# Merging TensorE runs in a fused attention and gated linear attention kernel, with every engine's order written anew

## The reference, cut to what matters

```python
x = x + xattn(layernorm(x), ctx, indices)      # x: 4 x 1024 x 256
x = x + ffn(layernorm(x))

# xattn: 16 heads of 16, 154 keys, 64 picks of keys per query (with repetition)
kv = (c_sel @ W_kv_up.T)                       # c_sel: picked rows of x_kv @ W_kv_down.T
attn = softmax(q k / 4 over the 64 picks);  out = (attn v) @ W_out.T

# ffn: 8 heads of 64, chunked gated linear attention
q1, k1, v = x @ Wq, x @ Wk, x @ Wv
q2 = x @ Wqa @ Wqb;  k2 = softmax(x @ Wka @ Wkb over 64)       # "second" keys
gk1, gk2 = log_sigmoid(x @ Wg1a @ Wg1b + b), log_sigmoid(x @ Wg2a @ Wg2b + b)
o = gla(q1, k1, v, gk1) + sum over 4 experts of gla(q2*f, k2*f, v, gk2*m)   # top-1 router
g = x @ Wga @ Wgb
o = o * rsqrt(mean(o*o) + eps) * norm_w * (g * sigmoid(g));  out = o @ Wo
```

## Time and profile before

| | |
|---|---|
| median of 3 runs | 1136.37 us (1136.36 to 1137.0) |
| profiled execution: its own time, its span | 1137.37 us, 1135.8 us |
| granted TensorE clock, mean | 0.988 |
| PE busy (matmul records) | 1077.7 us, 95% of the span, 11840 records |
| PE weight loads | 872.7 us, 77% |
| DVE busy | 978.7 us, 86% |
| ACT busy | 933.8 us, 82% |
| POOL busy | 686.0 us, 60% |

### The profile page before, as it was taken

How to read it: one execution, slowest core, us unless ns; L and a number is a source line. 1 busy time by engine, 2 the same in 40 slices (tenths; PEclk the granted TensorE clock), 3 DMA queues, 4 the chain that set the end, 5 groups by cost and what they waited for, 6 DMA issues and landing times.

```text
span 1135.8 us, 30935 instructions
## 1 busy us (share of the span) xinstructions
PE 1077.7 (95%) x11840; PEld 872.7 (77%) x11840; DVE 978.7 (86%) x2793; ACT 933.8 (82%) x2322; POOL 686.0 (60%) x707
## 2 busy tenths in 40 slices
PE   2879999999999999999999999999999999999986
PEld 1557888887888788778888887888787788888764
DVE  5679999998899999999999998999899999998652
ACT  2578888888888888888888898888889888888761
POOL 4266555577655556766655677565557666555553
PEclk9889999999999999999999999999999999999998
DMA  5432222223222222223212222222222222121111
GB/s 155 141 124 58 72 52 57 54 70 76 67 68 52 50 57 73 62 70 86 67 43 50 57 67 71 73 71 48 63 57 61 63 68 68 44 52 48 31 32 24
DMA packets 86857, 73.83 MB, mean 65 GB/s; under 512 B 34553, under 2 KB 71743, under 8 KB 86710
## 3 DMA queue, kind: packets, MB, share of 16 engines
q1 hardware_dynamic: 86278, 70.98, 24.4%
q10 hardware_dynamic: 432, 0.89, 0.2%
HBM read 37.43 MB, written 13.94 MB: 45 GB/s over the span
## 4 chain that ended last, share of the span: by engine, by line
PE 79%; DVE 8%; DMA 3%; POOL 3%; ACT 3%; SPq 2%; issue 1%; DVEq 0%; ACTq 0%
PE F L407 8%; PE F L862 5%; PE F L810 5%; PE TM L732 5%; PE F L401 5%; PE F L873 4%; PE F L782 4%; PE F L837 4%; PE TM L739 3%; PE F L797 3%; PE F L867 3%; PE SA L720 3%; PE F L821 3%; PE TM L749 3%; PE F L755 2%; PE F L854 2%
## 5 line engine op out<-in xcount | busy, mean ns | idle before, releaser
L727 DVE CUSTOM_DVE_ANT_0 SA<-SA,LNC 128x154 f32<-128x154 f32 x512 | 146.5, 346 | 16.2 <-PE SA L720 13.0
L2176 POOL TENSOR_TENSOR QREST<-QT,QPARTS 128x256 f32<-128x256 f32 x27 | 18.1, 672 | 174.6 <-ACT QPARTS L1872 174.6
L713 DVE TENSOR_REDUCE PACKED<-HOT 128x19 int32<-128x1216 bf16 x64 | 92.4, 1443 | 0.2
L2194 POOL TENSOR_TENSOR QM<-QD,ISEXPT 128x1024 f32<-128x1024 f32 x27 | 81.9, 3032 | 11.5 <-DMA QD<-QG 11.1
L732 PE MATMUL TM<-CONST,EXPS 128*128 128x128 f32 x512 | 84.5, 288 | 0.4 <-ACT OT L1781 0.4
L732 PEld LDWEIGHTS TM<-CONST,EXPS 128*128 128x128 f32 x512 | 73.9, 207 | 2.0 <-ACT OT L1781 0.7
L2166 POOL TENSOR_TENSOR LS<-LS,ZABS 128x1024 f32<-128x1024 f32 x27 | 64.0, 2371 | 13.5 <-ACT ZABS L1932 13.0
L727 DVE DVE_READ_ACCUMULATOR2_ANT MAXS<- 128x1 f32 x512 | 70.6, 138 | 0.0
L2174 POOL TENSOR_TENSOR LS<-LS,ZABS 128x512 f32<-128x512 f32 x27 | 34.5, 1279 | 54.9 <-ACT ZABS L1840 54.9
L720 PE MATMUL SA<-KNOW,QS 128*128 128x154 bf16 x512 | 56.0, 232 | 10.9 <-DMA KNOW<-k_dram 9.2
L407 PEld LDWEIGHTS F<-XMT,WQ 128*128 128x128 f32 x512 | 63.4, 196 | 2.7 <-issue 1.3
(11 more groups left out here) (541 smaller groups left out, 3813.2 us busy)
## 6 DMA issues: line engine op xcount, KB each, us to landing
QD<-QG SPq DMA_DIRECT2D x128, 128.0 KB, 2.3
QS<-q_dram SPq DMA_DIRECT2D x64, 192.0 KB, 3.3
q_dram<-QPARTS SPq DMA_DIRECT2D x32, 192.0 KB, 2.4
XA<-x_dram SPq DMA_DIRECT2D x32, 128.0 KB, 2.1
QS<-q_dram SPq DMA_DIRECT2D x32, 128.0 KB, 3.3
XB<-x_dram SPq DMA_DIRECT2D x32, 128.0 KB, 3.2
out_dram<-OUT SPq DMA_DIRECT2D x32, 128.0 KB, 1.7
EG<-EGP SPq DMA_DIRECT2D x128, 4.0 KB, 1.8
```

Source lines behind the costliest of these rows:

```text
L713: return dve.tensor_reduce(PACKED[:, r], HOT[:, r, :], AX.X, ALU.add)
L727: last = dve.tensor_tensor_reduce(s, s, LNC[t % 2][:, :], -1.0, LARGE, ALU.add, ALU.min, out[:, h:h + 1])
L2194: pool.tensor_tensor(QM[:, 1, :, :, :].rearrange("p a b t -> p (a b) t"), QD[:, :, :, :].rearrange("p a b t -> p (a b) t"), ISEXPT[d % 2][ ...
```

## The change

Two pairs of PE runs are merged, a few dependencies are bent to allow it, and all lists are ordered anew.

- `values_pair(b, 0)` and `values_pair(b, 2)` take the place of four `values`: 16 matmuls in one run, into 256 columns of TM (`OUTS2`) instead of 128. ACT copies a pair to OT with one instruction of 256 columns instead of two of 128. The pair needs both PT[0] and PT[1].
- `half_pairs_rows` does the gate features and the second keys in one run. The keys now go to the other half of the same two banks (`KIDS`). The copy to SG and the chain behind it (Abs, Relu, Exp, Ln, L2174's addition) move from the middle of turn c to its end and into turn d.
- The waits of `gate_products` on Q1 and of KG1T on the WK products fall away; the transposes of XM, ahead of it, now begin the turn, and they wait for XM, which DVE makes after Q1.
- In DVE's list XN goes from before the state additions to behind X1; HOT's multiplication from the stretch between `inner` runs to ahead of QG2; the reciprocal KS, KS3, K2's multiplication and the copy to PT[0] go from ahead of QG2 to behind it. In the steady turn `inner(KG1T, Q1)` still waits for QG2, `inner(KG2T, QG2)` for AT1, `kv_products` for AT2, `state_outputs` for QM (now for both halves).

The number of matmuls, of DVE's and of POOL's instructions stays the same; ACT has two instructions fewer in a turn.

```diff
-        OUTS = MA[:, 3 * P:4 * P]
+        OUTS2 = MA[:, 2 * P:4 * P].rearrange("p (n t) -> p n t", t=P)
-        MID, MIDS, MIDD = D2[:, 0:D], F[:, 0:2, 0:D], F[:, 2:4, 0:D]
-        k2_heads = MIDS.rearrange("p a (h d) -> p a h d", d=DK)
+        MID, MIDS, KIDS, MIDD = D2[:, 0:D], F[:, 0:2, 0:D], F[:, 0:2, D:2 * D], F[:, 2:4, 0:D]
+        k2_heads = KIDS.rearrange("p a (h d) -> p a h d", d=DK)
...
+        def values_pair(t, first):
+            v = VNOW[t // TPB % 2]
+            for n in range(2):
+                g, o, pt = first + n, OUTS2[:, n, :], PT[n]
+                for hh in range(GH):
+                    c = HA * VW + g * P + hh * VW
+                    pe.matmul(o[VW * hh:VW * hh + VW, :], v[:, c:c + VW], pt[:, cols(GH)],
+                              start=True, stop=False, skip_group_check=True)
+                for hh in range(GH):
+                    h = g * GH + hh
+                    last = pe.matmul(o[VW * hh:VW * hh + VW, :], v[:, h * VW:(h + 1) * VW], pt[:, cols(hh)],
+                                     start=False, stop=True, skip_group_check=True)
+            return last
...
+        def half_pairs_rows(pairs_out, rows_out, w_pairs, x0, x1, w_rows, y1, y0):
+            half_pairs(pairs_out, w_pairs, x0, x1)
+            return half_rows(rows_out, y0, y1, w_rows)
```

More of the change, by code:

```diff
@@ L733, in exp_transposes @@
             return pe.transpose(MA[:, 0:P], exps[:, P:NPAD, :].rearrange("p j h -> p (j h)"), ident)
[L735 to L740, removed]
-            for hh in range(GH):
-                h = g * GH + hh
-                last = pe.matmul(o[VW * hh:VW * hh + VW, :], v[:, h * VW:(h + 1) * VW], pt[:, cols(hh)],
-                                 start=False, stop=True, skip_group_check=True)
+        def values_pair(t, first):
[10 more added lines that the diff above has]
+                                     start=False, stop=True, skip_group_check=True)
             return last
@@ L1024, in pe_first_tiles @@
             if d >= 0:
+                pe.wait_ge(s_d_states, d + 1)
+                pe.wait_ge(s_d_sq, d + 1)
+                pe.matmul(D2, const("pairs"), RMS[:, :], start=True, stop=True).then_inc(s_d_ms_ps, 1)
+            if b >= 0:
+                pe.wait_ge(s_b_ot, 2 * b + 2)
+                transposes(TA, flat(OT[:, :, :]), GROUPS).then_inc(s_b_ot_ps, 1)
+            if d >= 0:
+                dense_kv_products(V[d % 2]).then_inc(s_d_kvd_ps, 1)
+            if c >= 0:
+                if c == 0:
+                    pe.wait_ge(s_vall, 2)
+                pe.wait_ge(s_c_hidg, 16 * c + 16)
+                pe.wait_ge(s_c_hidk, 16 * c + 16)
+                pe.wait_ge(s_c_by_label, c + 1)
+                half_pairs_rows(MIDS, KIDS, WG, HID2, HIDG, WKB, HID1, HIDK).then_inc(s_c_k2_ps, 1)
+            if b >= 0:
+                pe.wait_ge(s_b_out, 2 * b + 2)
+                transposes(TA, ON[:, :], KD).then_inc(s_b_ont_ps, 1)
+            if d >= 0:
                 if d == 0:
@@ L1104, in pe_tiles @@
             pe.wait_ge(s_b_probs_act, 2 * b + 2)
-            values(b, 3, PT[1]).then_inc(s_b_values, 1)
-            pe.wait_ge(s_c_router_y, 4 * c + 4)
+            values_pair(b, 2).then_inc(s_b_values, 1)
+            pe.wait_ge(s_c_router_y, 2 * c + 2)
+            pe.wait_ge(s_c_zmin, 2 * c + 2)
             router_rows().then_inc(s_c_rows_ps, 1)
+            pe.wait_ge(s_d_state1, d + 1)
+            pe.wait_ge(s_d_sq, d + 1)
+            pe.matmul(D2, const("pairs"), RMS[:, :], start=True, stop=True).then_inc(s_d_ms_ps, 1)
+            pe.wait_ge(s_b_ot, 2 * b + 2)
+            transposes(TA, flat(OT[:, :, :]), GROUPS).then_inc(s_b_ot_ps, 1)
+            dense_kv_products(V[d % 2]).then_inc(s_d_kvd_ps, 1)
+            pe.wait_ge(s_c_hidg, 16 * c + 16)
+            pe.wait_ge(s_c_hidk, 16 * c + 16)
+            pe.wait_ge(s_c_by_label, c + 1)
+            half_pairs_rows(MIDS, KIDS, WG, HID2, HIDG, WKB, HID1, HIDK).then_inc(s_c_k2_ps, 1)
+            pe.wait_ge(s_b_out, 2 * b + 2)
+            transposes(TA, ON[:, :], KD).then_inc(s_b_ont_ps, 1)
             if a % TPB == 0:
@@ L1252, in dve_first_tiles @@
+            if a >= 0:
+                dve.wait_ge(s_a_index_dve, a + 1)
+                dve.scalar_tensor_tensor(IW[5][:, :], IW[2][:, :], float(3 * BASES), IW[4][:, :], ALU.is_ge, ALU.add).then_inc(s_a_weights, 1)
+            if e >= 0:
+                dve.wait_ge(s_e_y_ps, e + 1)
+                dve.tensor_tensor(OUT[:, :], MID, X1B[e % 2][:, :], ALU.add).then_inc(s_e_out, 1)
             if b >= 0:
@@ L1534, in dve_last_tiles @@
+            dve.wait_ge(s_e_y_ps, e + 1)
+            dve.wait_ge(s_e_store, 16 * e)
+            dve.tensor_tensor(OUT[:, :], MID, X1B[e % 2][:, :], ALU.add).then_inc(s_e_out, 1)
             if c < TILES:
@@ L1962, in act_last_tiles @@
+                act.activation(ZABS[:, 2, :], ZABS[:, 2, :], ACT.Exp, scale=-1.0).then_inc(s_c_silu, 1)
             if b < TILES:
```

1487 lines of the change are left out of this document (701 added, 786 removed).

## The result

The changed kernel takes 1129.38 us (median, 1127.78 to 1129.8), the ratio to the kernel before is 0.9936 with an interval of 0.9919 to 0.9953: 7 us faster, where I had forecast 20. The direction and the range held, the size did not. The profiled execution, the fastest of the four, has a span of 1126.4 us against 1135.8.

A forecast was written before the change was run, and what follows sets the result against it. PE's runs bound the kernel at 32.98 us a turn; after the change the loop through DVE would, at 32.3. 27 x 0.68 = 18.4 plus 2 us made 20.4 less, 1116 us, range 1101 to 1140.

The forecast's parts named there:

- The step that failed: Pipeline start and end, apart from the full stages of turns 4, 5 and 33: nothing, between +3 and -3 us.
- my sum: Whole kernel: 27 x 0.68 = 18.4 us, and 2 us more from turns 4, 5 and 33, 20.4 less.
- The forecast of 32.3 us: Steady turn, set by the loop through DVE: 32.3 us, 0.68 less than 32.98; chance 0.45.
- DVE's stretch from STATE to QG2: DVE's list from the STATE addition to QG2's end: 16.32 us, net +0.45 from the moves, 16.77.
- My loop: STATE, DVE to QG2, PE's inner(KG1T) to the next state_outputs: 0.11 + 16.77 + 0.1 + 15.41 = 32.4 us, taken as 32.3.
- PE's sum: PE's runs per full turn: values -0.38, features and keys -0.57, WK -0.24, new neighbours +0.1: -1.1 us, turn 31.9.
- PE as the only bound: Rival, steady turn: the loop stays under 31.9 us and PE waits for nobody, 1104 us; chance 0.15.
- POOL as the bound: Rival: QM stays at 3.5 us, state_outputs waits 0.6 each turn, turn 32.8 or 32.9, 1132 us; chance 0.13.
- the waits eat the gain: Rival: merged runs need two producers each, turn stays within 0.1 of 32.98 us, 1136 us; chance 0.10.
- The slower case: Rival: POOL's L2174 addition holds DVE's XM, 1.35 us instead of 0.40, turn about 33.25, 1143 us; chance 0.17.

The follow-up runs named there:

- dve_more_before_qg2: Changed kernel, but in steady turns the reciprocal KS, KS3 and K2's multiplication stand ahead of QG2: 1166.3 us, turn 33.66 us.
- pe_less_pair2: Changed kernel, but in steady turns the second values pair leaves out the matmuls with the keys from 128 on: 1130.9 us, turn 32.20 us.
- four_values: Changed kernel, but in steady turns each values pair is split, first by two KG2T transposes, second by router_rows behind state_outputs: 1141.5 us, turn 32.68 us.
- pool_relief: Changed kernel, but in steady turns POOL's IW addition stands behind the second QM and QPARTS ahead of the second part of ZPARTS: 1131.2 us.
- both undoing runs: Changed kernel with values pairs split by other runs (1141.5 us), or with ON's transposes between gate features and second keys (1141.9 us).
- v_rest_early: Changed kernel with IDX's and ZW's loads early again and, in turn 3, PE's products for the rest of the values at the front: 1113.2 us.

## Why the prediction was wrong

**The step that failed** is "the rest of the start and the end waits for latencies, ...: nothing, between +3 and -3". It measured +13.3 up to the first ZW product, -1.4 in turns 4 and 5 and some -3 at the end. I had the new SP list and had reasoned about it for the steady turns only. In the turns that fill the pipeline each engine still has its setup in the list, and there the order of SP's list decides when a load starts. Three moves, of IDX, of ZW and of the products for the rest of the values, each put something short behind something long. With them undone the kernel takes 1113.2, 24 us less than before, where my sum had 20.4.

**The steady turn.** The forecast of 32.3 us and 27 x 0.68 = 18.4 came out: 32.20, and 18.2 over 26 turns. The mechanism came out in part. DVE's stretch from STATE to QG2 has next to no room: QG2's end is 0.16 us ahead of `inner(KG1T)`, and 0.06 where PE does wait for it (dve_more_before_qg2), so that loop has 0.1 to spare. The stretch was 16.3 and not 16.77, since the second scan and HOT's multiplication no longer stretch (1.44 against 1.69). But it does not come last, nor does it show as I had said: no row names QG2 or XM as what PE waits for. What comes last in a turn is DVE's answer right behind `state_outputs`: the STATE additions, for which the mean of squares waits, and OG*RMS, for which `ffn_out` waits. My loop has both on its DVE side, but it takes no account of PE being needed for the mean of squares in between. I read this from the distances of 0.055 us and from pe_less_pair2; no run made DVE's part there shorter. AT2's mask, QM and QG2 follow within about 0.1 us. So the added time lengthened the turn at four places (+0.48 at the first split, +0.42, +1.16, +1.46) and not at the second split of four_values, where PE would have waited, and taking 0.88 away gave 0.11. That 32.3 and 32.2 agree so well is in part luck, as the loop that I added up was not the last.

**PE's sum.** Its sizes hold. From start to start in the timelines of both kernels, in the median of the steady turns: the values take 2.02 and not 2.28, and T K2 and `v_product`, behind which two of them stood, 0.09 and 0.13 less, together 0.48, where I had 0.38. Features, keys and T ON in front of the keys take 1.35 and not 1.81, 0.46, where I had 0.57. WK takes 1.79 and not 2.03, 0.24 as written. Together 1.18 against my 1.19. PE's turn fell by 0.66, so the new neighbours give back 0.5, where I had put 0.1: the four `exp_transposes` 0.18 more, scores 0 0.12, `hidden` 0.09, T KG2T 0.10, `router_rows` with the wait for STATE 0.20, and others less.

**The rivals.** PE as the only bound falls: 0.88 less work of PE gave 0.11. POOL as the bound falls: QM takes 2.37 both times, and pool_relief gave nothing for the 0.12 us by which it made QM early. That the waits eat the gain falls in the steady turn, but waits for two late loads and for LS did eat most of it in the start, a place where I had not looked for them. The slower case did not come: XM takes 0.40 in all steady turns, and L2138's addition ends at 554.63, 0.04 ahead of XM. Its mechanism is real all the same: in dve_more_before_qg2 POOL's QREST holds KS3 in each steady turn, 0.69 against 0.23 us. It is in the changed kernel's trace too, at its start: XN, 0.40 in the steady turns, takes 2.19 beside a memset of POOL and ends 0.14 us behind it.

```profile
7.12 2.19 DVE L1244 TENSOR_SCALAR XN<-XA,MV,RSTD 128x256 f32<-128x256 f32 x1 [2.11 <-ACT RSTD L1771]
```

```profile
6.51 2.66 POOL L528 MEMSET VALL<- 128x3072 f32 x1
```

The Trainium skill, page "SBUF — State Buffer", section "SBUF: two separate sides", has this as an exclusive lock of a shared pair of ports, for POOL's instructions and for some kinds of DVE's; the traces agree (2.19 against 0.40 us, 0.69 against 0.23).

## What to carry to other kernels

A change that orders a whole pipeline anew has two prices, that of the steady turn and that of the filling: go through SP's list of the first turns load by load, and ask of each what stands in front of it and who waits. When an engine is busy 99% and nothing shows a wait, it need not be the bound: here its runs filled exactly the time of DVE's answers. A kernel with less work for PE told that, and so does the distance from DVE's end to PE's start, if it is the same in every turn and as short as where PE does wait. A turn that gets longer by the expected amount doesn't show that it did so for the expected reason: look which distances grew. An instruction ahead of an important one may be there to fill a gap: moving HOT's multiplication (1.37 us from start to start) behind QG2 made the turn 1.16 us longer.

## What the runs showed that I had not expected

A change of PE's array shape cost about 0.15 us of PE's time in both undoing runs (0.30 for two changes, of 128x32 tiles against whole and of 64x128 against whole), and none of the turn where PE was going to wait anyway. A DVE instruction of 8 columns, 0.23 us by itself, cost 0.69 when it began 0.01 us behind one of POOL's. The 0.3 us in front of `state_outputs` that the rows put down to POOL's QM is there with QM 0.12 us earlier as well (4.1 us over 13 turns, "issue"). The load of IDX, 32 KB, took 6.59 us behind the loads of QS and others, 2.0 in the median of all turns. And the stall had a second price: the granted clock was 0.54 between 75 and 100 us, where the kernel before had 0.86 and v_rest_early 0.92. Behind PE's idle time of 2.4 and 6.5 us it was at 0.50, the 1.2 GHz level, from 74 to 97.8 us. The kernel before and v_rest_early were there for some 10 us (72 to 82, 69 to 78.8). The halves of the values run stand 0.43 us apart at that level, 0.22 at the other. How much of the 13 us that is, no run takes apart.
